# A GRU and mixture kernel: its feature products as two matmuls of 64 columns of the PE array instead of four of 32

## The reference

```python
# block 0: input mixing, two GRU layers over 1024 time steps, gate, output
mixed = jnp.tanh(jnp.einsum('bte,he->bth', x, W_in) + b_in + ctx)
h1 = _gru_layer(mixed, Wih0, Whh0, bih0, bhh0)
h2 = _gru_layer(h1, Wih1, Whh1, bih1, bhh1)
gate = jax.nn.sigmoid(jnp.einsum('bh,gh->bg', context, W_gate) + b_gate)
gated = gate[:, None, :] * h2 + h2
return jnp.einsum('bth,eh->bte', gated, W_out) + b_out
# block 1: a shared unit and the two best of eight experts for each token
shared = jax.nn.silu(xf @ w1) * (xf @ w3) @ w2
h = jax.nn.gelu(jnp.einsum('nc,ech->enh', xf, W1e), approximate=False)
y = jnp.einsum('enh,ehc->enc', h, W2e)
routed = jnp.einsum('ne,enc->nc', combine, y)
```

## Time and profile before

| | us |
|---|---|
| median of 2 runs | 2396.11 (2394.64 to 2397.57) |
| profiled execution, its own time | 2396.67 |
| its span in the trace | 2394.9 |
| PE busy (47852 matmul records) | 2211.3 |
| PE weight loads busy | 1385.5 |
| VectorE busy | 2099.9 |
| ScalarE busy | 1371.4 |

### The profile page before, as it was taken

The page is one execution under the profiler, slowest core; times in us unless marked ns, Lnnn a source line. Parts: engine busy times, 40 slices in busy tenths (PEclk is TensorE's granted clock), DMA queues, the critical chain, the costliest instruction groups (busy, mean ns, idle before and its releaser), DMA issues.

```text
span 2394.9 us, 117959 instructions
## 1 busy us (share of the span) xinstructions
PE 2211.3 (92%) x47852; PEld 1385.5 (58%) x47852; DVE 2099.9 (88%) x13489; ACT 1371.4 (57%) x6577; POOL 41.4 (2%) x203
## 2 busy tenths in 40 slices
PE   6788999999999999999999999999999999999987
PEld 2445566656556556566656556556566656556555
DVE  4888889899898989989999898999989899998974
ACT  3555655656555565555655555565555655565552
POOL 0000000000000000000000000000000000000000
PEclk9999999999999999999999999999999999999999
DMA  5000000000000000000000000000000000000000
GB/s 199 2 2 3 3 5 3 3 6 3 5 3 3 6 3 6 3 5 3 3 5 3 5 3 3 5 3 5 3 3 5 3 5 3 5 3 4 5 3 7
DMA packets 8483, 21.47 MB, mean 9 GB/s; under 512 B 1265, under 2 KB 5377, under 8 KB 7681
## 3 DMA queue, kind: packets, MB, share of 16 engines
q1 hardware_dynamic: 7936, 13.93, 1.6%
HBM read 11.83 MB, written 2.10 MB: 6 GB/s over the span
## 4 chain that ended last, share of the span: by engine, by line
DVE 67%; ACT 17%; PE 9%; issue 6%; DMA 0%; SPq 0%; DVEq 0%; ACTq 0%
ACT z_th L438 17%; DVE n_first L358 15%; DVE cells L385 13%; DVE r_pre L357 13%; DVE cells L376 12%; DVE z_pre L359 7%; PE bank L305 7%; DVE hid L594 3%; PE bank L255 2%; DVE n_second L345 1%; DVE hid L582 1%; ACT cells L440 1%; DVE x L550 0%; DVE mid L579 0%; DVE hist L393 0%
## 5 line engine op out<-in xcount | busy, mean ns | idle before, releaser
L305 PE MATMUL bank<-w_h,cells 128*22 128x192 f32 (+4 forms) x32768 | 1773.5, 334 | 170.5 <-DVE cells L385 125.2
L305 PEld LDWEIGHTS bank<-w_h,cells 128*22 128x22 f32 (+4 forms) x32768 | 891.6, 117 | 876.9 <-DVE cells L385 758.0
L436 ACT ACTIVATE n_second<-r_pre 128x4 f32<-128x4 f32 x2048 | 427.2, 209 | 874.9 <-DVE r_pre L357 866.2
L358 DVE STREAM_TRANSPOSE n_first<-bank 128x64 f32<-128x64 f32 x2048 | 531.1, 259 | 0.2
L357 DVE STREAM_TRANSPOSE r_pre<-bank 128x64 f32<-128x64 f32 x2048 | 471.9, 230 | 41.8 <-PE bank L305 41.1
L376 DVE TENSOR_SCALAR cells<-z_th 128x4 f32<-128x4 f32 x2048 | 352.4, 172 | 151.8 <-ACT z_th L438 0.4
L438 ACT ACTIVATE z_th<-z_pre 128x4 f32<-128x4 f32 x2048 | 421.0, 206 | 110.7 <-DVE z_pre L359 0.9
L385 DVE TENSOR_TENSOR_SCAN cells<-cells 128x23 f32<-128x23 f32 x2048 | 412.2, 201 | 43.2 <-DVE hist L393 0.2
L440 ACT ACTIVATE cells<-n_scan 128x4 f32<-128x4 f32 x2048 | 431.4, 211 | 0.2 <-DVE n_scan L367 0.2
L359 DVE STREAM_TRANSPOSE z_pre<-bank 128x64 f32<-128x64 f32 x2048 | 427.1, 209 | 0.0
L367 DVE TENSOR_TENSOR_SCAN n_scan<-n_first,n_second 128x12 f32<-128x12 f32 x2048 | 374.3, 183 | 26.8 <-ACT n_second L436 0.9
(11 more groups left out here) (84 smaller groups left out, 600.7 us busy)
## 6 DMA issues: line engine op xcount, KB each, us to landing
x_t<-in_x_t SPq DMA_DIRECT2D x4, 512.0 KB, 6.4
w_1e<-in_w_1e SPq DMA_DIRECT2D x1, 2048.0 KB
w_2e<-in_w_2e SPq DMA_DIRECT2D x1, 2048.0 KB
out_y<-y SPq DMA_DIRECT2D x16, 128.0 KB, 2.2
w_x<-in_w_x SPq DMA_DIRECT2D x2, 768.0 KB, 7.6
w_h<-in_w_h SPq DMA_DIRECT2D x2, 768.0 KB, 9.3
w<-in_w SPq DMA_DIRECT2D x3, 512.0 KB
w_in<-in_w_in SPq DMA_DIRECT2D x1, 256.0 KB, 2.4
```

The lines of the kernel that those rows point to most:

```text
L305: mm = pe.matmul(gates[l][p][32 * g:32 * g + B * (j + 1), 0:3 * U], state_tile(l, j, kt), w_h[l][:, kt, g, :], start=False, stop=False, ti ...
L358: v.transpose(n_first[l][:, :, :, 2].rearrange("p i b -> p b i"), blocks(gates[l][p][:, 0:U])).then_inc(s["for_n"], 1)
L436: act.activation(n_second[l][p][:, own, :, 0], r_pre[l][:, own], ACT.Tanh, scale=0.5).then_inc(s["for_n"], 1)
```

## The change

`by_columns` issues two matmuls instead of four. Each has 64 stationary columns instead of 32, at the array columns 0 and 64, and writes 64 PSUM partitions. `recur`, `project` and `place_biases` keep their four matmuls of 32 array columns. All waits, all semaphores and the order of the work on every engine stay.

```diff
         def by_columns(pe, ps, w, x, start, stop):
 
-
-            for g in range(NQ):
-                strip = slice(32 * g, 32 * g + 32)
-                mm = pe.matmul(ps[strip], w[:, strip], x, start=start, stop=stop, tile_position=(0, 32 * g),
+            for g in range(2):
+                half = slice(64 * g, 64 * g + 64)
+                mm = pe.matmul(ps[half], w[:, half], x, start=start, stop=stop, tile_position=(0, 64 * g),
                                skip_group_check=True)
             return mm
```

## The result

The changed kernel takes 2449.11 us (median of 2 runs, 2448.24 to 2449.98) against 2396.11: ratio 1.022, 95% interval 1.0196 to 1.0245. It is slower by 53 us. The sign and the place were as forecast, but 2520 us, a loss of 124, was 2.3 times too much. The time lies at the very bottom of the forecast's own range of 2445 to 2620 us.

What follows compares the result with a forecast made beforehand. One layer's loop of 2.17 us was taken to bound the kernel; width changes lengthen half slots from 1.124 to 1.20 us, x 1600 = +122 us on 2397, so 2520 us. Its own range was 2445 to 2620, the range with rivals 2390 to 2660.

Steps and rivals of the forecast that it cites:

- What bounds the kernel: One layer's loop over PE, DVE and ACT, 2.17 us, sets half slots of at least 1.09 us; products have room.
- Removed instructions count as 0: In the products, 6464 fewer matmuls and as many loads save at most a few ns, none on the chain.
- A change of width waits for the last matmul of the other width, to 0.07 us before its recorded end: On PE, 32 to 64 columns and back, twice in every half slot with a product; loads start 0.07 us before the end.
- the one row at the start of the program: The trace's only width change, 128 to 8 columns: the load came 0.14 us late, 0.07 before the last matmul's end.
- Rival 1: Width changes on PE cost nothing, or hide in the idle 0.3 us; 2390 to 2425, say 2397 us; chance 0.34.
- rival 2: Each width change on PE drains fully to the recorded ends; half slot 1.32 us, total 2705 us; chance 0.17.
- rival 3: With half the instructions products leave the array earlier and recurs start earlier; at most 14 us, 2383 us; chance 0.02.
- PE's need: PE time from one recur's first load to the next one's, in a half slot with a product: 1.17 us, taken as 1.20.
- the second wide load exposed: In a product, the second pass's wider load not covered by the first's stream: 0.03 us more, making 1.20 us.
- A half slot of 1.124 us becomes 1.20: +0.076 us x 1600: Each of the 1600 mixture products lengthens its own half slot in the steady part; +122 us in all.
- Input mixing costs nothing: The 14 or so mixing products in the loop have 0.46 us of idle PE behind them, against about 0.3 needed.
- The signs to look for: Profile signs if right: product loads about 0.8 us behind the recur's, idle port towards none, about 333 steps, PE share over 30%.

Runs made afterwards that it cites:

- The run with two of 32: Changed kernel with each mixture product as two matmuls of 32 columns, at columns 0 and 64, half of it left out; 2398.21 us, ratio 0.9999.
- the control: Four matmuls of 32 columns as in the kernel before, each mixture product streaming only 64 of its 128 tokens; 2400.63 us, ratio 1.0017.

## Why the prediction was right or wrong

**What bounds the kernel.** Right. The run with two of 32 and the control show products off the path; 64 columns with 64 tokens, whose need fits under the loop, cost no more than that control.

**Removed instructions count as 0.** Right, by the run with two of 32.

**A change of width waits for the last matmul of the other width, to 0.07 us before its recorded end.** Right, from the one row at the start of the program and to about 0.01 us: 0.06 to 0.08 in both directions in the steady part. Of the 1493 places in the trace where a product of 64 follows a recur, the load starts 0.071 or 0.072 us before the recorded end in every one. Rival 1 (no price, 0.34), rival 2 (full drain to the recorded ends, 0.17) and rival 3 (faster, 0.02) fall. The doubt whether a row taken while matmuls ran slower holds for the steady part is settled: it does.

**PE's need, 1.17 us, "and 1.20 with the second wide load exposed as well. I take 1.20".** This is the first step that failed. The product takes 0.44 us, so the need is 0.865 - 0.07 + 0.44 - 0.07 = 1.165 us (1771.3 / 2048 = 0.865 is the recur). The loads of the two passes, 0.135 each, span 0.20 with both tiles, and the second ended before the first pass had (a matmul record of 64 columns takes 0.296). With 64 columns I had the load right (140 forecast) and its exposure wrong; even the loads of 128 columns were covered. By my own sum that is 0.035 x 1600 = 56 us of the 71 that I was too high. (The terms that I gave add up to 1.176, not 1.17; against the measured 1.165 that is a matter of 0.01 us.)

**"A half slot of 1.124 us becomes 1.20: +0.076 us x 1600", and half slots with a projection or nothing "stay at 1.09 to 1.14".** This is the second. With the right need the sum is 0.041 x 1600 = 66 us and the measurement 53. The half slots without a product did not stay: one layer's loop spans two half slots and needs 2.17 us in both together, so a half slot behind a long one may be shorter than 1.09. The load port of the changed kernel around a projection:

```profile
1214.20 0.48 PEld L304 LDWEIGHTS bank<-w_h,cells 128*14 128x14 f32 x16 [0.17 <-DVE cells L384]
...
1215.36 0.51 PEld L304 LDWEIGHTS bank<-w_h,cells 128*22 128x22 f32 x16 [0.17 <-DVE cells L384]
1215.89 0.29 PEld L285 LDWEIGHTS bank<-w_x,stage 128*32 128x32 f32 x8
1216.37 0.48 PEld L304 LDWEIGHTS bank<-w_h,cells 128*16 128x16 f32 x16 [0.19 <-DVE cells L384]
```

1.16 us with a product, then 1.01 with a projection: 2.17 together. The traces of before and after, added up from each recur's first load to the next one's, show how the 53 us come about. 1480 half slots with mixture products take 69.5 us more in all (1.141 us on average before, 1.188 after). The 250 with a projection take 13.2 us less (1.125 before, 1.072 after), and the rest 3.0 less. What is given back is thus 16 us. The count was off too: 1480 half slots of the loop hold mixture products and not 1600, since some hold two and the last products come behind the last recur. The same overstatement shows with 128 columns (need 1.215, sum 146 us, measured 110) and with 96 tokens.

**Input mixing costs nothing.** Right: 2399.88 us.

**The signs to look for.** The product's load started 0.78 us behind the recur's (0.8 forecast), PE's share of the chain rose to 55% (well over 30), the load took 135 ns (140). Two signs failed. Half slots with a projection went down to 1.01 us and did not stay at 1.09 to 1.16. The port's idle time before recurs shrank from 0.3 us only to 0.17, and is still put down to the scan. And 348 steps were counted where I had 333; but 333 is every half slot at 1.20, which does not fit my own sum, with 448 of them shorter.

## What to carry to other kernels

Keep all small matmuls that alternate on TensorE at one width of the array, even if that means four instructions in place of two or of one: here the loads of four strips of 32 could start while the recur's last matmuls still ran, and those of wider tiles could not. In these runs such a wait was free as long as the need of the engine, with both waits in it, stayed below the period that another loop set, so work out the need first and compare it with that period. When two loops interleave, sum over a loop and not over its halves, and when a cost is bounded by an overlap that a row shows (two loads within one pass), do not add it a second time for caution.

## What the runs showed that I had not expected

The wait at a change of width ended 0.07 us before the recorded end of the last matmul whatever the widths: 128 to 8 at the start, 32 to 64, 64 to 32, and 128 to 32. The ends of matmuls are modelled, so 0.07 us is a distance in the profile's terms. And 8 columns behind a recur were no change of width at all. The routing product of the changed kernel, which has 8 columns and no `tile_position`, starts its loads 0.34 us before the recur's recorded end (221.85 + 0.86):

```profile
221.85 0.86 PE L304 MATMUL bank<-w_h,cells 128*18 128x192 f32 x16 [0.26 <-DVE cells L384]
...
222.37 0.47 PEld L540 LDWEIGHTS bank<-x,w_r 128*8 128x8 f32 x4
```

What counts is thus not the number of columns itself: 2 to 32 columns (recurs and routing) behaved as one width, and 64 and 128 as others than that. No run puts 64 beside 128.

The runs with shortened products, the control and the one with 64 columns and 64 tokens, were 3 to 4 us slower than before, though the products were not on the path. The control's granted clock was 0.78 in the last 95 us, where the kernel before had 0.96, and 1.00 from 240 to 2300 us in both. Stretches of PE, of the control:

```profile
240.00:2300.00 2060.00, 1804.51 (x42676) 1.00 0.02 4
2300.00:2395.00 95.00, 63.74 (x1792) 0.78 0.02 4
```

In that stretch layer 0 has run out of steps, and PE is busy for 63.74 of 95 us where it was 70.11 before. The mean of 0.78 means that it spent part of the stretch at the lower of its two levels, 1.2 GHz. The traces of the control and of the kernel before place the whole difference there. Up to the 2021st step (by the first turn of each step) the control is 0.9 us ahead of the kernel before; the last 27 steps take 59.9 us against 52.6, and what is behind them takes 2.8 us less. That the clock is the cause of the longer steps is likely, and was not tried by itself.
